# Graph layer on one core: gathers land in buffers of their own and are copied on by ScalarE; table tiles go ahead of the late product on TensorE

## The reference

```python
seg = lambda v: jax.ops.segment_sum(v, dst, num_segments=n)
xs = x[src]
deg_w = jnp.maximum(seg(edge_weights), 1.0)
deg_c = jnp.maximum(seg(jnp.ones_like(edge_weights)), 1.0)
norm = edge_weights / jnp.sqrt(deg_w[src] * deg_w[dst])
gcn = seg(norm[:, None] * xs) @ Wgcn + bgcn
sage = x @ Wsage_s + seg(xs) / deg_c[:, None] @ Wsage_n + bsage
agg_w = seg(edge_weights[:, None] * xs)
gin = ((1.0 + gin_eps) * x + agg_w) @ Wgin + bgin
gconv = x @ Wgc1 + agg_w @ Wgc2 + bgc
eop = seg(edge_weights[:, None] * jax.nn.relu(xs + edge_attr)) @ Wedge + bedge
return jnp.einsum('k,knd->nd', weights, jnp.stack([gcn, sage, gin, gconv, eop]))
# the layer's output: layernorm(x + the above)
```

## Time and profile before

| | us |
|---|---|
| time, median of 3 runs | 2230.78 (2224.48 to 2244.31) |
| profiled execution, its own time | 2228.75 |
| its span | 2226.9 |
| PE busy | 1556.4 (70%) |
| POOL busy | 1355.2 (61%) |
| DVE busy | 928.6 (42%) |
| ACT busy | 826.9 (37%) |
| mean granted clock of TensorE | 0.867 of full speed |

### The profile page before, as it was taken

How to read it: one execution, slowest core, us unless ns; L and a number is a source line. 1 busy time by engine, 2 the same in 40 slices (tenths; PEclk the granted TensorE clock), 3 DMA queues, 4 the chain that set the end, 5 groups by cost and what they waited for, 6 DMA issues and landing times.

```text
span 2226.9 us, 22565 instructions
## 1 busy us (share of the span) xinstructions
PE 1556.4 (70%) x6037; PEld 1007.5 (45%) x6037; DVE 928.6 (42%) x2539; ACT 826.9 (37%) x1201; POOL 1355.2 (61%) x1426
## 2 busy tenths in 40 slices
PE   1004367566888777877878778777887888877876
PEld 1003367553554544544445445444444445544546
DVE  5684256543433332433433433243333334423346
ACT  1676233243433433424244234233333324423323
POOL 7665366556666656656666666566666656665660
PEclk9999967688989888978889888888888888888988
DMA  5111234331222222222222222222222222222223
GB/s 98 23 24 51 70 100 112 95 80 42 51 64 45 55 54 46 57 46 44 54 57 53 47 57 43 47 58 50 48 66 43 48 51 57 47 53 44 59 55 77
DMA packets 83186, 126.12 MB, mean 57 GB/s; under 512 B 29494, under 2 KB 31269, under 8 KB 82821
## 3 DMA queue, kind: packets, MB, share of 16 engines
q0 software_dynamic: 45056, 48.85, 13.6%
q1 hardware_dynamic: 36371, 74.90, 11.0%
q10 hardware_dynamic: 1650, 1.04, 0.2%
HBM read 121.29 MB, written 3.40 MB: 56 GB/s over the span
## 4 chain that ended last, share of the span: by engine, by line
PE 43%; issue 18%; another core or an unknown queue 17%; DVE 10%; ACT 4%; POOL 3%; DVEq 2%; DMA 1%; SPq 0%; POOLq 0%; ACTq 0%
PE psum L1280 27%; PE psum L1261 13%; ACT ring L604 4%; POOL ring L559 3%; DVE ring L1076 2%; DVE sums L1065 2%; DVE early L988 1%; PE psum L1312 1%; PE psum L1228 1%; DVE attr L953 1%; DVE early L992 1%; DMA ring<-node_table,idx 1%; PE psum L1341 1%; PE psum L1342 1%
## 5 line engine op out<-in xcount | busy, mean ns | idle before, releaser
L559 POOL DMA_INDIRECT ring<-node_table,idx x1280 | 1228.4, 960 | 758.2 <-issue 389.4
L1280 PE MATMUL psum<-table_sb,early_x 128*128 128x455 f32 x2240 | 988.1, 586 | 115.6 <-issue 110.1
L1280 PEld LDWEIGHTS psum<-table_sb,early_x 128*128 128x128 f32 x2240 | 446.0, 205 | 573.4 <-issue 566.7
L1261 PE MATMUL psum<-ring 128*128 128x120 f32 x2560 | 405.3, 313 | 246.5 <-issue 127.5
L1261 PEld LDWEIGHTS psum<-ring 128*128 128x128 f32 x2560 | 375.5, 224 | 310.2 <-issue 164.9
L988 DVE TENSOR_TENSOR early<-psum,digit_hot 128x455 f32<-128x455 f32 x160 | 100.6, 631 | 989.5 <-remote 599.3
L688 ACT ACTIVATE early_x<-early,minus_ids 128x256 f32<-128x256 f16 x560 | 370.4, 744 | 138.7 <-remote 103.4
L655 ACT ACTIVATE ring<-attr 128x512 f32<-128x512 f32 x160 | 100.2, 626 | 483.4 <-DVE attr L953 383.8
L679 ACT ACTIVATE early<-early 128x256 f32<-128x256 f32 x40 | 16.7, 416 | 518.2 <-DVE early L1009 385.1
L1065 DVE TENSOR_TENSOR sums<-sums,psum 64x40 f32 (+1 forms) x648 | 127.5, 197 | 97.4 <-remote 53.6
L526 POOL DMA_INDIRECT early_x<-in_x,early_idx x128 | 122.0, 953 | 61.4 <-issue 40.3
(11 more groups left out here) (158 smaller groups left out, 644.8 us busy)
## 6 DMA issues: line engine op xcount, KB each, us to landing
attr<-in_edge_attr SPq DMA_DIRECT2D x79, 512.0 KB
ring<-node_table,idx POOLq DMA_INDIRECT x1280
early<-in_edge_attr SPq DMA_DIRECT2D x36, 256.0 KB
src_all<-in_src SPq DMA_DIRECT2D x16, 512.0 KB
early<-key_rows SPq DMA_DIRECT2D x10, 512.0 KB
early_x<-degree_rows SPq DMA_DIRECT2D x2, 1568.0 KB
early_x<-in_x,early_idx POOLq DMA_INDIRECT x128
node_table<-table_sb SPq DMA_DIRECT2D x1, 1666.0 KB, 6.0
```

What stands on the lines that cost most here:

```text
L559: nc.gpsimd.indirect_dma_start(out=feat[:, u, j, D:BLOCK], out_offset=None, in_=table, in_offset=bass.IndirectOffsetOnAxis(ap=idx[:, u, j: ...
L1261: last = nc.tensor.matmul(to[:, 0:3 * WINDOW], features[:, j, 0:2 * D], hots[:, j].rearrange("p k n -> p (k n)"), start=(j == 0), stop=(j ...
L1280: last = nc.tensor.matmul(pick_ps[k % 2].rearrange("p (b c) -> p b c", b=SPLIT), node_hot[:, k, a], table_sb[:, a * SPLIT:(a + 1) * SPLIT, ...
```

## The change

- The gathers no longer write `feat`. Each place u has a `landing` (128 partitions x 8 x 68): two are new, two lie in `scratch`. `feat` becomes narrower, 2 x 64 columns for each tile.
- ScalarE copies the 64 features of each row from `landing[u]` to `feat[:, u, :, D:2 * D]` after `summed_in`, ahead of the Relu, and counts `lifted`.
- POOL waits for `lifted` (of slot k-4) instead of `chunk_product`, and, ahead of the gathers for place 2, for `windows_set`.
- DVE reads `landing[u]` for the root column and the sum, and waits for `lifted` ahead of `window()`.
- In the turns TensorE runs `pick_tile` ahead of `late_chunk`. The early steps and the plain slots keep their order.

```diff
--- before.py
+++ after.py
@@ -116,9 +116,9 @@
         row_w = area[:, 4 * CHUNK:6 * CHUNK].rearrange("p (g e) -> p g e", g=2)
 
         attr = sb("attr", [P, UNROLL, TILES, D])
-        FEATS, HOTS = UNROLL * TILES * BLOCK, UNROLL * TILES * 3 * WINDOW
+        FEATS, HOTS = UNROLL * TILES * 2 * D, UNROLL * TILES * 3 * WINDOW
         ring = sb("ring", [P, FEATS + HOTS])
-        feat = ring[:, 0:FEATS].rearrange("p (u j b) -> p u j b", u=UNROLL, b=BLOCK)
+        feat = ring[:, 0:FEATS].rearrange("p (u j b) -> p u j b", u=UNROLL, b=2 * D)
 
         hot = ring[:, FEATS:FEATS + HOTS].rearrange("p (u j k n) -> p u j k n", u=UNROLL, k=3, n=WINDOW)
         attr_flat = attr[:, :, :, :].rearrange("p u j b -> p (u j b)")
@@ -138,6 +138,9 @@
         e_win = sb("e_win", [P, CHUNKS, TILES], BF16)
 
         scratch = sb("scratch", [P, CHUNKS * TILES])
+        landing_free = sb("landing", [P, UNROLL // 2, TILES, TROW])
+        landing = [landing_free[:, k] for k in range(UNROLL // 2)] + [
+            scratch[:, k * TILES * TROW:(k + 1) * TILES * TROW].rearrange("p (j b) -> p j b", b=TROW) for k in range(UNROLL - UNROLL // 2)]
         e_tmp = scratch[:, :].rearrange("p (c j) -> p c j", j=TILES)
         e_w = sb("e_w", [P, CHUNKS, TILES])
 
@@ -302,6 +305,7 @@
         hots_ready = sem("hots_ready")
         summed_in = sem("summed_in")
         relu_ready = sem("relu_ready")
+        lifted = sem("lifted")
         chunk_product = sem("chunk_product")
         early_idx_loaded, early_gathered = sem("early_idx_loaded"), sem("early_gathered")
 
@@ -553,11 +557,13 @@
                     for u in range(UNROLL):
                         it = v * LATE + i * UNROLL + u
                         pool.wait_ge(staged, v * (LATE // 2) + i * (UNROLL // 2) + u // 2 + 1)
-                        pool.wait_ge(chunk_product, it + 1)
+                        pool.wait_ge(lifted, it + 1)
+                        if u == UNROLL // 2:
+                            pool.wait_ge(windows_set, v + 1)
                         pool.sem_inc(gathers_begun, 1)
                         for j in range(TILES):
                             nc.gpsimd.indirect_dma_start(
-                                out=feat[:, u, j, D:BLOCK], out_offset=None, in_=table,
+                                out=landing[u][:, j], out_offset=None, in_=table,
                                 in_offset=bass.IndirectOffsetOnAxis(ap=idx[:, u, j:j + 1], axis=0),
                             ).then_inc(gathered[u], 16)
 
@@ -637,6 +643,7 @@
                     lift_x(k + 2)
 
             act.sem_inc(relu_ready, UNROLL)
+            act.sem_inc(lifted, UNROLL)
             act.sem_inc(early_relu_ready, 1)
             act.sem_inc(distance_ready, 1)
             act.sem_inc(relu_g, 2)
@@ -652,6 +659,7 @@
                         act.wait_ge(gathered[u], (v * LATE_STEPS + i + 1) * (16 * TILES))
                         nc.scalar.copy(idx[:, u - 1:u + 1], e_src[:, bass.ds((i + 1) * UNROLL + u - 1 + BASE, 2)]).then_inc(staged, 1)
                     act.wait_ge(summed_in, v * LATE + i * UNROLL + u + 1)
+                    nc.scalar.copy(feat[:, u, :, D:2 * D], landing[u][:, :, 0:D]).then_inc(lifted, 1)
                     nc.scalar.activation(feat[:, u, :, 0:D], attr[:, u], ACT.Relu).then_inc(relu_ready, 1)
 
                 def far_sources(c):
@@ -933,6 +941,7 @@
             link(nc.vector.memset(win_off[:], 0.0))
             with dve.Fori(0, n_pass) as v:
                 dve.wait_ge(early_gathered, early_landed(v))
+                dve.wait_ge(lifted, v * LATE + UNROLL)
                 window(v, 0)
                 nc.vector.tensor_copy(w_late[:, UNROLL - 1], e_w[:, BASE])
 
@@ -947,10 +956,10 @@
                         nc.vector.tensor_copy(w_late[:, 0:n], e_w[:, bass.ds(c, n)])
                     window_hots(hot[:, u], e_win[:, c])
                     dve.wait_ge(gathered[u], turn * (16 * TILES))
-                    nc.vector.tensor_tensor(out=wroot[:, u], in0=e_w[:, c], in1=feat[:, u, :, 2 * D], op=ALU.mult)
+                    nc.vector.tensor_tensor(out=wroot[:, u], in0=e_w[:, c], in1=landing[u][:, :, D], op=ALU.mult)
                     loaded = (v * (LATE_STEPS + 1) if u > 1 else v * LATE_STEPS) + i + 1
                     dve.wait_ge(attr_loaded[u // 2], (loaded + (u > 1 and last)) * 16)
-                    nc.vector.tensor_tensor(out=attr[:, u], in0=attr[:, u], in1=feat[:, u, :, D:2 * D],
+                    nc.vector.tensor_tensor(out=attr[:, u], in0=attr[:, u], in1=landing[u][:, :, 0:D],
                                             op=ALU.add).then_inc(summed_in, 1)
 
                 def weigh_hots(i, u):
@@ -1294,9 +1303,9 @@
                     for m in range(TURN_CHUNKS * SLOTS):
                         i, u = EARLY_STEPS + s * TURN_STEPS + m // UNROLL, m % UNROLL
                         c, r = s * TURN_CHUNKS + m // SLOTS, m % SLOTS
-                        late_chunk(i, u)
                         for half, k in tiles_of(r):
                             pick_tile(2 * c + half, k)
+                        late_chunk(i, u)
                         if r == 5:
                             unit_product(2 * c, 0)
                         if r == 1 and (begun or m > SLOTS):
```

## The result

| | before | after |
|---|---|---|
| median, us | 2230.31 | 2563.61 (2557.13 to 2570.69, 4 runs) |
| ratio to before | | 1.149 (95%: 1.144 to 1.154) |
| profiled execution's span, us | 2226.9 | 2560.9 |
| granted clock of TensorE | 0.867 | 0.794 |

The change makes the kernel 15% slower here. The direction was forecast, the size was not: 333 us in place of 58, and beyond the range.

A forecast was written before the change was run, and what follows sets the result against it. It took POOL's gather bursts and pauses to set the pace, with neither TensorE nor POOL full. The terms summed as 2228.75 + 122 - 50 - 12 = 2289 us, with an 8-in-10 range of 2100 to 2410.

The forecast's parts named there:

- The mechanism: Across engines: long unbroken runs of POOL's gathers slow the others, which recover when POOL pauses; no size of its own.
- I take 13.0, because the new wait makes this the ordinary end of a burst: POOL's new wait, slots 20 to 159: 13.0 us for each slot instead of 12.12, +122 us.
- The four cycles behind the 13.0: Old-trace cycles where POOL already ended on the index copy: ten slots in 129.75 us, 13.0 each.
- The early steps: Slots 4 to 20, already at 12.9 us each: no added time taken.
- The order: TensorE's turns, tile ahead of late product: -50 us, half of the bounds 0 and -105.
- ScalarE's copy at 0: New copy ahead of the Relu on ScalarE: 100 us of work, costed at 0, up to +100 without cover.
- The start: Wait for `windows_set` ahead of slot 2 cuts the first burst from 32 to 16 gathers: -12 us.
- That the pattern stays: Rival: POOL goes on in pairs, pausing some 3.7 us after each as before; 2167 us, chance 24%.
- POOL becomes the bound: Rival: POOL never stops between gathers, 9.99 us each slot; 1921 us, chance 16%.
- no change: Rival: the ring ends bursts as products did, longer bursts eat the order's saving; 2229 us, chance 14%.

The follow-up runs named there:

- e3: Changed kernel, with POOL also waiting for the product of four slots back, as well as for the lift: 2223.10 us, ratio 0.994.
- e4: Changed kernel, with POOL waiting after each slot's eight gathers until they have landed: 2292.03 us, ratio 1.026.
- e8: Changed kernel, with three POOL memsets in place of each late gather, landings staying zero: 1872.40 us.
- e2: Changed kernel with TensorE's old order put back, late product first and tile second: 2515.01 us, ratio 1.121.
- e1: Kernel before, with only TensorE's order changed, tile ahead of the late product in the turns: 2212.88 us, ratio 0.990.
- e13: Kernel before, unchanged, run again for its trace in the other surroundings: 1830.30 us.
- e7: Changed kernel, with a short POOL memset and a wait for it after every gather: 2943.95 us, ratio 1.32.

## Why the prediction was right in its direction and wrong in its size

- **The mechanism** ("a long unbroken run of gathers slows the other engines' progress, and they recover when POOL pauses") held, with a correction: it is TensorE that is slowed, not ScalarE and DVE. e3, e4 and e8 show it. That removing the product's wait lets bursts grow to 24 and 32, which ScalarE then ends, came as said, and it is the index copy that ends them.
- **The failed step** is "I take 13.0, because the new wait makes this the ordinary end of a burst". It measured 14.01: +262.6 us in place of +122 (and of +72 with the order's -50, which is in the measured figure); with the landings alone (e2) it is 13.86. The four cycles behind the 13.0 held 16 and 24 gathers, the longest that the old wait let through. Bursts of 24 cost 13.3 us for each slot after, near the estimate, but 13 bursts of 32 cost 14.8, and they alone are 93 of the 140 us between 13.0 and 14.01. I had named bursts of 32 in the last part of the prediction, with pauses of 6 to 9 us, and took the price of shorter ones for them; the pauses were 10.1 us behind 24 and 19.5 behind 32.
- **The early steps** ("at 12.9 already, I take nothing") were +48.3 us. It is a second step that failed. Their bursts before were mostly of eight gathers with pauses of 2.2 to 2.8 us; after they are of 16 with pauses of 8 to 10 us. The tail behind slot 159, of which the prediction has no term, added 20 us, with a burst of 32 in it.
- **The order**, -50 us, was half right alone (-21 in e1; the wait fell as forecast), and wrong in sign beside the landings (+48).
- **ScalarE's copy at 0** was near: 10 us with the landings in e3.
- **The start**, -12 us, was +3.5. The first burst was not cut to 16 but came late, since I put the initial count of `lifted` at nothing. That count (L646) stands in ScalarE's program behind the setup's copies:

```profile
235.62 1.04 DVE L842 TENSOR_SCALAR scratch<-e_dst,win_off 128x1568 f32<-128x1568 f32 x1 [1.48 <-ACTq L646]
...
236.39 1.39 POOL L565 DMA_INDIRECT landing<-node_table,idx  x1 [50.00 <-ACTq L646]
```

POOL stood 50.00 us for it, until 236.39 instead of 204.66, and by slot 2 `window()` was long done, so that the first burst ran on to 48 gathers. TensorE and ScalarE met no gathers there, and DVE's window began 20.7 us earlier than before, as the argument wanted; POOL used the gain up.
- **The rivals.** That the pattern stays was wrong. "POOL becomes the bound" was wrong where I predicted, and is what both kernels do in the other surroundings, at the 9.99 us given there (the rows behind it, 1065.02 us and 1112 times 0.30, rather make 10.06); since the kernel before does it as well, nothing is gained. In the other surroundings the result is no change, which I gave 14% for another reason.

- **The two rules.** The advice to double-buffer and overlap DMA with compute ("Trainium Kernel Development and Optimization" in the Trainium skill, Best Practices) is followed by this change, and the runs give 0.9997 for it in one surroundings and 1.149 in the other: the measurement decides. The clock went the way of the section on HAM oscillation ("TensorE: Matmul & The Clock Gate" in the Trainium skill): with longer waits the granted clock fell from 0.867 to 0.794, and it is 0.936 in e13, where TensorE is not held up. It falls as far with waits of another cause: in e7, where TensorE is not held up but stands for POOL's slow gathers, it is 0.796.

## What to carry to other kernels

A wait can be what keeps an engine from harming others, though it was written for a buffer: before it is removed, look at what the others do while the waiting engine works without a pause, and price the longest run that the new wait allows, not the longest in the old trace. Put the old wait back next to the new mechanism (one line here): it tells at once which part of a change costs. And a cause of this kind may not be there on the next machine: take the kernel before again beside each comparison, and its trace when its time has moved.

## What the runs showed of the hardware

With an indirect gather of POOL each 1.25 us, in some surroundings, TensorE runs at full rate for a while (15.5 us in the burst shown, 12 to 21 in the 31 bursts of 24 and 32 of the changed kernel), then issues matmuls singly, up to 3 us apart, until some 5 us after the last gather of that burst. Its counts reach DVE late, in that burst 13 and 24 us behind the tile's last matmul (the longest wait of DVE for a tile was 35.8 us). DVE and ScalarE go on answering each other at once. It hardly depends on the bytes (a quarter: 2544.61 us) or the rows (half: 2599.50), is gone with a gather each 2.0 us and nearly so with pauses of 2.7 us after eight, stays with a rest of 0.8 us after eight, and is not there with memsets in the gathers' place. In other surroundings 1280 gathers in one run do no harm, and the kernel before takes 1830 us instead of 2230. It is not a matter of more traffic: the page of e13 has the same 83,186 packets as that of the kernel before, 53 and 56 of them instructions. What holds TensorE up, and what differs between the surroundings, no run shows.
